# The rows of h that a unit multiplies: from DRAM instead of turned by TensorE

## The reference, cut to what matters

```
h   = concat(pool_1(x), pool_2(x)) @ w5 + b5            # (B, 300)
g   = sum over r of v[i, r] * v[j, r]                   # one number for each pair i < j
f7  = sum over pairs i < j of g[i, j] * h[:, i] * h[:, j] * w7[pair, :]   # 44850 pairs, (B, 300)
out = (h @ w6 + b6) @ w8a + (f7 + b7) @ w8b + b8        # (B, 300)
z   = label_embedding (B, 200, 300) dotted with out, and dense_ctx (B, 16)
y   = relu(relu(z @ top1) @ top2) @ top3                # (B, 1)
```

## Time and profile before

| | |
|---|---|
| median of 3 runs (lowest, highest) | 1901.45 us (1899.33, 1904.08) |
| the profiled execution's own time | 1906.87 us |
| its span, first to last instruction | 1905.0 us |
| PE matmuls busy | 1692.2 us (89%) |
| DVE busy | 1679.8 us (88%) |
| ACT busy | 1033.0 us (54%) |
| POOL busy | 562.6 us (30%) |
| DMA | 563.23 MB, mean 296 GB/s |
| mean granted TensorE clock | 0.961 |

### The profile page before, as it was taken

How to read it: one execution, slowest core, us unless ns; L and a number is a source line. 1 busy time by engine, 2 the same in 40 slices (tenths; PEclk the granted TensorE clock), 3 DMA queues, 4 the chain that set the end, 5 groups by cost and what they waited for, 6 DMA issues and landing times.

```text
span 1905.0 us, 26074 instructions
## 1 busy us (share of the span) xinstructions
PE 1692.2 (89%) x7104; PEld 1246.1 (65%) x7104; DVE 1679.8 (88%) x5837; ACT 1033.0 (54%) x3216; POOL 562.6 (30%) x413
## 2 busy tenths in 40 slices
PE   0168989999999999999999999999998999997751
PEld 0145657777777777777777777767776777775531
DVE  0889988998999989999999999999997889867685
ACT  0458767486457554456554674455753544454534
POOL 6757161854610061700058107700000000000053
PEclk9789999999999999999999999999998999999975
DMA  6528895665987869897878856899648999989985
GB/s 192 188 65 297 272 344 163 203 233 170 364 347 296 308 221 406 326 373 286 319 261 306 330 198 233 339 407 355 229 174 349 410 367 386 395 310 419 419 329 235
DMA packets 97795, 563.23 MB, mean 296 GB/s; under 512 B 16437, under 2 KB 16682, under 8 KB 72052
## 3 DMA queue, kind: packets, MB, share of 16 engines
q1 hardware_dynamic: 78356, 499.91, 68.9%
q0 software_dynamic: 19280, 61.67, 10.2%
q10 hardware_dynamic: 16, 0.00, 0.0%
HBM read 561.52 MB, written 0.00 MB: 295 GB/s over the span
## 4 chain that ended last, share of the span: by engine, by line
PE 50%; DVE 31%; DMA 10%; issue 4%; ACT 3%; SPq 2%; POOL 1%; DVEq 0%; ACTq 0%; POOLq 0%
PE acc L853 42%; DVE junk L558 15%; DVE qa L600 8%; DVE prod L639 7%; DMA w_sb<-in_w 6%; DMA lab<-in_labels 3%; SPq L471 2%; PE coarse L708 2%; PE acc L840 1%; PE acc L773 1%; PE misc L780 1%; ACT heads L964 1%; DMA z<-in_ctx 1%; PE acc L755 1%; PE acc L758 1%
## 5 line engine op out<-in xcount | busy, mean ns | idle before, releaser
L853 PE MATMUL acc<-w_sb,prod 128*128 128x300 f32 (+2 forms) x5680 | 1535.2, 420 | 56.6 <-DMA w_sb<-in_w 35.1
L853 PEld LDWEIGHTS acc<-w_sb,prod 128*128 128x128 f32 (+2 forms) x5680 | 1044.0, 191 | 407.7 <-issue 49.1
L1031 ACT ACTIVATE prod<-prod,g_all 128x256 f32<-128x256 f32 (+3 forms) x1625 | 691.0, 470 | 489.0 <-DVE prod L639 486.6
L502 POOL DMA_INDIRECT x<-in_tbl,ids_sb x376 | 496.3, 1320 | 708.2 <-DVE qa L600 593.6
L639 DVE TENSOR_TENSOR prod<-fine,coarse 128x1280 f32<-128x1280 f32 (+4 forms) x325 | 424.3, 1311 | 89.4 <-PE coarse L708 87.6
L558 DVE SCALAR_TENSOR_TENSOR junk<-lab,out 128x300 f32<-128x300 f32 x1056 | 424.5, 464 | 21.5 <-DMA lab<-in_labels 21.3
L558 DVE SCALAR_TENSOR_TENSOR junk<-x,score_u 128x300 f32<-128x300 f32 x752 | 303.6, 467 | 0.1
L600 DVE SCALAR_TENSOR_TENSOR qa<-x,ex,qa 128x300 f32<-128x300 f32 x674 | 303.1, 521 | 0.0
L536 POOL TENSOR_TENSOR x<-x,out 128x2400 f32<-128x2400 f32 x6 | 31.5, 5264 | 602.4 <-ACT out L939 592.7
L964 ACT ACTIVATE heads<-x 128x300 f32<-128x300 f32 x376 | 152.2, 405 | 0.4 <-ACT y_sb L878 0.3
L558 DVE SCALAR_TENSOR_TENSOR junk<-x,out 128x300 f32<-128x300 f32 x344 | 137.7, 465 | 0.0
(11 more groups left out here) (86 smaller groups left out, 606.5 us busy)
## 6 DMA issues: line engine op xcount, KB each, us to landing
w_sb<-in_w SPq DMA_DIRECT2D x325, 750.0 KB, 6.7
lab<-in_labels SPq DMA_DIRECT2D x140, 1200.0 KB, 8.5
x<-in_labels SPq DMA_DIRECT2D x60, 1200.0 KB, 9.3
x<-in_tbl,ids_sb POOLq DMA_INDIRECT x376, 5.2
prod<-in_v_i SPq DMA_DIRECT2D x1, 710.0 KB
prod<-in_v_j SPq DMA_DIRECT2D x1, 710.0 KB
w_sb<-in_w SPq DMA_DIRECT2D x1, 709.0 KB
top_sb<-in_top SPq DMA_DIRECT2D x1, 512.0 KB
```

The costliest lines, as they stand in the source:

```text
L502: pool.indirect_dma_start(out=row_of(t, n), out_offset=None, in_=tables[n], in_offset=bass.IndirectOffsetOnAxis(ap=ids_sb[:, t, n:n + 1], ...
L853: last = pe.matmul(acc[:, t % 3, 0:EMB], prod[0:rows, u % RING, m, t % 2 * P:(t % 2 + 1) * P], w7_sb[0:rows, u % W7_RING, m * EMB:(m + 1) ...
L1031: act.activation(chunk, chunk, ACT.Copy, scale=g_all[0:rows, pair:pair + 1]).then_inc(chunk_ready, 1)
```

## The change

TensorE makes h already turned: `make_h` has `w5` as the stationary operand and the turned q as the moving one, and gives three blocks of 100 components by 128 examples. ACT copies them to `ht` (a ring of three) and writes them to DRAM, into `h_pairs`: for each pair of tiles that can be active together, 448 rows (h once and a half) of 256 examples. Each tile is written to the two pairs that it belongs to, by three transfers each. `turn_coarse`, `turn_fine`, `pick_window`, `repeat_fine`, `copy_fine`, their semaphores and buffers and PE's turning of h for the output (in `turn_f7`) go. In their place ACT issues one load for each unit, four units ahead, and five loads for each part, one a tick, from the fourth unit before it. They wait for the stores of the active tiles. `coarse` now is in SBUF, in a ring of four.

```diff
+COARSE_RING = 4
+HT = 3
-CROSS, UNIT, GATHER, LOAD_W7, LOAD_SLAB = (0, 8, 14), (0, 29, 57), 70, 20, 33
+CROSS, UNIT, GATHER, LOAD_W7, LOAD_SLAB = (0, 8, 14), (0, 28, 54), 70, 20, 33
+FINE_LOADS = {(u - 4) * FINE + m: (u, m) for u in range(1, TOTAL) if begins_part(u) for m in range(FINE)}
+        ht = sb("ht", [P, HT, ECN * P])
+        h_pairs = nc.dram_tensor("h_pairs", (TILES - 1, HH, 2 * P), F32).ap()
...
             def make_h(t):
-                dst = scratch(t)[:, 0:EMB]
-                for c in range(QCN):
-                    rows = QC + (c == QCN - 1)
-                    last = pe.matmul(dst, qt[0:rows, c * P:(c + 1) * P], w5_sb[0:rows, c, :],
-                                     start=c == 0, stop=c == QCN - 1)
+                for m in range(ECN):
+                    for c in range(QCN):
+                        rows = QC + (c == QCN - 1)
+                        last = pe.matmul(scratch(t)[0:EC, m * P:(m + 1) * P],
+                                         w5_sb[0:rows, c, m * EC:(m + 1) * EC], qt[0:rows, c * P:(c + 1) * P],
+                                         start=c == 0, stop=c == QCN - 1)
...
-                    if m == 0 and u + 2 < TOTAL:
-                        turn_coarse(u + 2)
...
+            def store_h(t):
+                for pair in pairs_of(t):
+                    columns_of = slice(t % 2 * P, (t % 2 + 1) * P)
+                    act.dma_start(h_pairs[pair, 0:EMB, columns_of].rearrange("(c p) b -> p c b", p=EC),
+                                  ht[0:EC, t % HT, :].rearrange("p (c b) -> p c b", c=ECN)).then_inc(h_stored, 16)
+                    act.dma_start(h_pairs[pair, EMB:EMB + EC, columns_of],
+                                  ht[0:EC, t % HT, 0:P]).then_inc(h_stored, 16)
+                    act.dma_start(h_pairs[pair, EMB + EC:HH, columns_of],
+                                  ht[0:HH - EMB - EC, t % HT, P:2 * P]).then_inc(h_stored, 16)
+            def h_rows(u, start, *rows):
+                slot, n = slots_of(u)
+                first = h_pairs[pair_of(u), start:start + 1, slot * P:(slot + n) * P]
+                return bass.AP(tensor=first.tensor, offset=first.offset,
+                               ap=[[step * 2 * P, count] for step, count in rows] + [[1, n * P]])
+            def load_coarse(u):
+                phase, k = phase_of(u)
+                slot, n = slots_of(u)
                 if phase < 2:
+                    src = h_rows(u, P * phase + FINE * k + 1, (1, P))
                 else:
                     start, windows, width = ((2 * P + THIRD, COARSE, LEFT), (2 * P, 3, THIRD))[phase - 2]
+                    src = h_rows(u, start + windows * FINE * k + 1, (FINE, windows), (1, width))
+                act.wait_ge(h_stored, 16 * stores_upto(max(active(u))))
+                act.dma_start(coarse[0:rows_of(u), u % COARSE_RING, slot * P:(slot + n) * P],
+                              src).then_inc(coarse_loaded[u % COARSE_RING], 16)
+            def load_fine(u, m):
+                phase, _ = phase_of(u)
+                slot, n = slots_of(u)
+                if phase < 2:
+                    src = h_rows(u, (EMB, P)[phase] - m, (1, P))
+                else:
+                    start, width = ((2 * P + THIRD, LEFT), (2 * P, THIRD))[phase - 2]
+                    src = h_rows(u, start - m, (0, rows_of(u) // width), (1, width))
+                place = part_count(u) % PLACES
+                act.wait_ge(h_stored, 16 * stores_upto(max(active(u))))
+                act.dma_start(fine[0:rows_of(u), place, m, slot * P:(slot + n) * P],
+                              src).then_inc(fine_loaded[place], 16)
...
-                    if m == 1 and u + RING < TOTAL:
-                        pick_window(u + RING)
+                    if m == 1 and u + COARSE_RING < TOTAL:
+                        load_coarse(u + COARSE_RING)
                     tick = u * FINE + m
+                    if tick in FINE_LOADS:
+                        load_fine(*FINE_LOADS[tick])
```

More of the change, by code:

```diff
@@ L99, in slots_of, with pair_of, pairs_of, stores_upto @@
     return slots[0], len(slots)
-def hh_at(t):
-    return t % 2 * 2 + t // 2 % 2
+def pair_of(u):
+    return min(min(active(u)), TILES - 2)
+def pairs_of(t):
+    return [pair for pair in (t - 1, t) if 0 <= pair < TILES - 1]
+def stores_upto(t):
+    return sum(3 * len(pairs_of(n)) for n in range(t + 1))
 def gathers(t):
@@ L256, in schedule @@
     at = {}
-    for u in range(1, TOTAL):
-        if begins_part(u):
-            first = u - (9 if phase_of(u)[0] == 2 else 5)
-            for n in range(FILLS):
-                at[(first + n) * FINE + 2] = ("fill", u, n)
     for t in range(TILES):
@@ L285, in schedule @@
             copies.setdefault(tick - 2, []).append(("f7s", of, 0))
[L286 to L288 removed]
+        copies.setdefault(tick + 3, []).append((name, of, n))
     return at, end, copies
 BURSTS, END_BURSTS, COPIES = schedule()
+FINE_LOADS = {(u - 4) * FINE + m: (u, m) for u in range(1, TOTAL) if begins_part(u) for m in range(FINE)}
 def dlrm_tower(nc, ids, tables, labels, ctx_in, w_score, b_rep, w5, w6, b7_in, w7, w8a_in, w8b,
@@ L346, in dlrm_tower @@
         qt = big[:, 0:QCN * P]
-        f7t, ht = (big[:, n * ECN * P:(n + 1) * ECN * P] for n in range(2))
+        f7t = big[:, 0:ECN * P]
         ones = big[96:P, (QCN - 1) * P:2 * ECN * P]
@@ L635, in cross @@
                 slot, n = slots_of(u)
-                window = coarse[0:rows, u % 2, slot * P:(slot + n) * P]
+                window = coarse[0:rows, u % COARSE_RING, slot * P:(slot + n) * P]
                 window = bass.AP(tensor=window.tensor, offset=window.offset,
@@ L843, in _ @@
                 burst(name, of, n, 0)
-            for u in range(2):
-                turn_coarse(u)
             for u in range(TOTAL):
@@ L891, in pick_window @@
-                if u >= RING:
-                    act.wait_ge(coarse_ready, u - RING + 1)
-                act.activation(out, cols, ACT.Copy).then_inc(picked_ready, 1)
-            def repeat_fine(u, n):
-                phase, _ = phase_of(u)
-                slot, tiles = slots_of(u)
-                start, width = ((2 * P + THIRD, LEFT), (2 * P, THIRD))[phase - 2]
-                times = PHASE_ROWS[phase] // width
-                for m in range(2 * n, min(2 * n + 2, FINE)):
-                    cols = hh_cols(u, start - m, [0, times], [1, width])
-                    copy(dup[:, m % 2, slot:slot + tiles, 0:times * width].rearrange(
-                        "p t (k n) -> p t k n", k=times), cols)
@@ L905, in copy_fine @@
-            def copy_fine(u, n):
-                rows = rows_of(u)
-                slot, tiles = slots_of(u)
-                ms = range(2 * n, min(2 * n + 2, FINE))
-                made = misc[0:rows, 0:len(ms) * 2 * P].rearrange("p (m b) -> p m b", b=2 * P)
-                act.activation(fine[0:rows, part_count(u) % PLACES, ms[0]:ms[-1] + 1,
-                                    slot * P:(slot + tiles) * P],
-                               made[:, :, slot * P:(slot + tiles) * P], ACT.Copy).then_inc(fine_ready, 1)
+                    src = h_rows(u, start + windows * FINE * k + 1, (FINE, windows), (1, width))
@@ L1019, in _ @@
                         sum_abs(1, n)
-                if name == "h":
-                    for u in range(RING):
-                        pick_window(u)
+            for m in range(FINE):
+                load_fine(0, m)
+                if m < COARSE_RING:
+                    load_coarse(m)
             act.wait_ge(g_ready, 2)
```

99 lines of the change are left out of this document (22 added, 77 removed).

## The result

The changed kernel takes 2080.88 us (median of 4 runs, 2073.84 to 2084.97) where before takes 1902.76 us beside it: ratio 1.0933, interval 1.0893 to 1.0974. The forecast was 1983 us with a range up to 2070; the side is right, and the size about half (83 of 178 us); the terms at the end show what of it was right. The profiled execution has a span of 2075.1 us.

What follows compares the result with a forecast made beforehand. No single engine bounds it; PE, DVE and the DMA engines are each near their limit somewhere. Span 1905 - 25 + 73 + 30 + 5 = 1988 us, less 5 us from profiled execution to median: 1983 us, range 1885 to 2070.

Steps and rivals of the forecast that it cites:

- PE's relief: On PE, removed transposes minus dearer `make_h` free 76 us net; a gain of 25 us was taken, bounds 10 and 43.
- something for DVE, which is as full as PE and stops part of the lead: Unsized deduction from PE's 43 us gain: DVE's 87.6 us of waiting are all that it can give.
- the second rival: DVE takes all that PE gives, with evenly spread loads: gain 5 us, total 1914 us; chance 8%.
- where the DMA share stays near one and a faster PE only asks for w7 sooner: In the last 450 us PE's relief doesn't count: 11 us off the 43 us gain.
- ScalarE and the evenly cut loads: ACT's removed copies against its added issues: zero; at the end, evenly cut coarse and fine loads: 10 us.
- Even: On ACT, 462 added DMA issues at 0.33 us, 151 us, balance the removed copies, including 121.5 and 26.7 us.
- Three engines for a phase-3 load: Phase-3 loads run on three DMA engines, 42 rows each: 73 us in the stretches and 20 us at the end.
- The third rival: The three engines serve rows alternately with w7 or slab rows: about 150 us more, 2133 us; chance 12%.
- Stores: Storing h to DRAM on ten engines, with later loads waiting for it: 5 us in all, bounds 0 and 7 x 8.
- The first load that waits for them is a unit (5.3 us) later: Stores of h take 2.8 us for two pairs, w7 rows between them more; the first dependent load comes 5.3 us later.
- Plan costs: New costs in `plan()` only let crosses come a little earlier in DVE's order: 0, with 10 us either way.
- The end: From 1700 us on bytes set the time: phase-3 loads add 20 us, other coarse and fine loads 10, nothing hides them.

Runs made afterwards that it cites:

- e10: Changed kernel with old plan costs and no h traffic after the first tile's stores and first loads, in a second-kind set: ratio 0.9907 to before.
- e18: Changed kernel with only the old plan costs restored, phase-3 loads not split: 2067.14 us, ratio 1.0871 to before.
- e15: Changed kernel with old plan costs and each phase-3 load split into three loads of 42 rows: 2002.59 us, ratio 1.0531 to before.
- e16: The kernel of e10 (changed, old plan costs, no h traffic after the start) run again in a first-kind set: 1898.92 us, ratio 0.9977 to before.
- e6: The changed kernel run again with no further edit, in a second-kind set: ratio 1.0644 to before.
- e7: The kernel before, run again unchanged with its profile in a second-kind set: ratio 0.9997 to before.

## Why the prediction was wrong

**PE's relief: -25 us forecast, -3.8 measured, ScalarE's relief with it.** The failed step is "something for DVE, which is as full as PE and stops part of the lead". In units 71 to 97 it stopped nearly all of it, so the second rival's mechanism was right there, and 8% too little for it. The step before it failed too: the forecast took 11 us off for the last 450 us, "where the DMA share stays near one and a faster PE only asks for w7 sooner", and just there (units 254 to 284, at a share of 1.00) the gain of 10.6 us came. Why it was lost again in three other stretches is open. In the other kind of sets the same removal gained 20 us (e10).

**ScalarE and the evenly cut loads: 0 and 10 us forecast, +57 measured for the loads' presence and lateness, some 9 of it stores.** The failed step is "Even", and two things in it failed. The price: not 151 us of issues but 399, since 0.33 us was the price of one on SP's queue, and in bunches single ones took 0.83 to 0.95 us, three took 1.24 to 1.62, and a held one up to 14.76. And the place: the issues of a part's fine and coarse loads come together, just where the units are short and their chunks are waited for.

**Three engines for a phase-3 load: right, +73 and 20 forecast, +64.6 measured.** Splitting the same rows over three loads takes back 3.4 points and ends DVE's waits for coarse loads (65.8 us in e18, 1.8 in e15). The place was right as well: the five stretches give 9.2, 13.5, 20.6, 12.5 and 9.6 us between e15 and e18, 65.4 in all. The trace agrees with the rule cited from the Trainium skill (DMA: Bandwidth & Descriptors, "Why a DMA increments its semaphore by 16 and not by 1") for a count of three on the source side: the rows start in threes. From before to the changed kernel the stretches grew by 20.5, 24.4, 19.7, 29.8 and 25.6 us, 120 in all, over the 50 us at which the forecast would have fallen, and over the sum of 93 because the stores and the presence of the loads lie in them too. That the size came so near is in part luck, since the price went by work alone. The third rival's mechanism was right: a row of h waits behind one row of w7 or of a slab (0.25 or 0.39 us, 0.23 or 0.36 forecast), so that 42 rows take some 17 us. What was said against it, that SP's queue runs empty when units stand still, failed: its share was 98.5% from 1510 to 1540 us while PE worked 15.2 of 30 us, with three slabs and two w7 blocks issued meanwhile. Its price of 150 us more didn't come. Four units of lead (some 20 us) can hide one such load, which would explain it, but no run tests this. The Trainium skill (DMA: Bandwidth & Descriptors, "Queues, rings and completion order") lets an engine take a packet of typically 9 to 17 descriptors from one queue before it turns to the next; the records here show turns of a single row.

**Stores: 5 us forecast, bounds 0 and 56, +46.5 measured.** The step "The first load that waits for them is a unit (5.3 us) later" had the stores land in 2.8 us. In e15 the first load that reads a tile's h was issued 3.6 to 34.9 us after the first of its stores, and the wait stood on ScalarE, in front of the chunks. With the 9 us of the second tile the stores cost some 55: the bound held, and the value chosen within it was at the wrong end.

**Plan costs: "0, with 10 either way" forecast, +13.7 measured here, +19 and +31 elsewhere.** It is the difference of two large terms that I had not looked for: +68 us at the end (153.8 instead of 86.0), where 21 slabs more wait behind the last unit with nothing beside them, and 54 us back where they lay before (units 71 to 97: 135.8 us instead of 149.6).

**The end: +20 and 10 forecast.** The place was wrong: units 310 to 324 grew by 22 us between e16 and e18, as loads on three engines and issues; behind the last unit nothing was lost to them (86.0 us in e18, 89.8 before).

So the terms -25 (relief), 10 (the even loads), 5 (stores), 93 (three engines) and 0 (costs) became -4, 57, 46, 65 and 14. The sum is 178 instead of 83 by the loads' presence and the stores (104 us against 15), by the gain that didn't come and by the costs; the three engines, 28 us under their 93, took part of it back.

## What to carry to other kernels

A DMA issue takes its engine's queue and doesn't show in its busy time: put new issues and above all new waits on an engine whose next instruction nobody is waiting for, and look at the densest stretch, not at the sum. Read a load's outermost count before its bytes: with three, its 42 rows stand one by one behind the rows of the large queue. Before a gain on one of two nearly full engines is counted, read the other's busy time in the same window. Costs in a planner that shift work to the end are judged with both sides, the end they lengthen and the stretch they relieve.

## What the runs showed of the hardware

**Two queues on one DMA engine, row by row.** The rows of a load with an outermost count of three start in threes, never with more than three under way, and about 0.4 us apart while SP's queue has rows of w7 and slabs for the same engines (1510 to 1540 us of the changed kernel).

**A second kind of run.** In the sets where before takes 2058 to 2072 us, other engines stand still while GpSimd issues its second burst of gathers. The waits between 150 and 240 us in e10 there:

```profile
ACT ht L840 <- remote: 58.9, 1, 58.9
```

PE had made this h by 167.5 us, GpSimd's last gather of the burst began at 217.9, and the copy began at 224.9. In the first kind ScalarE copies h while the gathers run, and the first cross comes at 148.6 us (e16) and not at 234.0. Before's head is longer there by 62 us (208.2 instead of 146.0) and the changed kernel's by 85. Yet the change costs less there, 1.064 instead of 1.093, because behind its head before loses another 100 us and the changed kernel only 20 (its units 183 to 213 take 181.9 us in e6 and 186.7 in the first kind, before's 192.2 in e7 and 175.4). What makes the two kinds is open, and so is why an engine stands still.
